# Score rows and centre norms from one product of the pooled sums, and a new order of every engine's list

## The chip, the cores and the metric

The kernel runs on one core of one Trainium2 chip. The metric is the device time of one execution in microseconds (us). The engines are TensorE (PE, with its weight loads shown apart as PEld), VectorE (DVE), ScalarE (ACT), GpSimd (POOL) and SyncE (SP, which issues the DMAs). They run their own instruction streams in order and meet at semaphores.

## The reference, cut to what matters

The input x has 32 images of 96 channels and 56 by 56 pixels. One layer is a clustering "convolution" and a quantised feed-forward part, each with a residual:

```
xn = x normalised over channels
f, v = Wf xn + bf, Wv xn + bv            # 8 heads of 48 channels
per quarter image (28x28 pixels) and head:
    centers = mean of f over 4x4 blocks of 7x7 pixels        # 16 centers
    cos(m, n) = f(n).centers(m) / (|f(n)| |centers(m)|)
    sim = sigmoid(beta + alpha * cos), kept for the best center of a pixel only
    agg(m) = (sum_n sim(m,n) v(n) + mean v) / (sum_n sim(m,n) + 1)
    out(n) = sum_m sim(m,n) agg(m)
x = x + Wp out + bp
t = x + FFN(normalised x)                # weights by sign, activations scaled by the
                                         # largest magnitude of a group of images
```

Pooling is linear, so the sums of xn over a block (with a constant row for the bias), call them s, give centers = Wf s. A score row is q = Wf^T (Wf s) = G s with G = Wf^T Wf for each head, and the squared length of a center is s^T G s = q.s. The groups of the feed-forward part are five groups of six images; the last two images have no feed-forward part.

## The kernel before, in words

A quarter image (784 pixels, 7 tiles of 112) is the unit of work. A group has 24 quarters. A first pass over them does the clustering part and the first half of the feed-forward part (normalise, transpose, the hidden product and its largest magnitude). When the largest magnitude of the whole group is known, a second pass over 48 half quarters recomputes the hidden product, applies GELU and the second weight, and leaves y on the chip. The final step of a group (clip y, scale it, add it to the image and store it) is done during the first pass of the next group. So the program is: setup, then five times a first and a second pass, then a last part with the eight quarters of the last two images and the final step of the fifth group. The final step is therefore in the first pass of groups 1 to 4 (counted from 0), and not in that of group 0.

The first pass is a software pipeline written by hand. `attention` of each engine is a list of steps, and `pipeline` runs the list once for each slot j. An entry is (phase, lag, step) and works on quarter j - lag + phase, with the phases X = 4 (normalise x, pool it, make score rows), M = 3 (features and their norms, scores), A = 2 (sigmoid, masking, aggregate, project, spread, residual) and R = 0 (feed-forward and final step). The order of the list is the order in which an engine issues. The entries marked FFN, FINAL and FILL are left out where a part has no such work.

For the score rows the kernel before goes this way: `pooled` (DVE) sums xn over blocks into cenx; `centers` (PE, L915) multiplies by wfT into 96 rows for each of four pairs of heads; `centers` (DVE, L656) copies that with a mask for the two heads into cbd; `center_squares` (POOL, L391) squares it into csq; `center_products` (PE, L923) sums the squares over rows by a product with ones and multiplies cbd by wf to get the 128 score rows; `center_floor` (DVE, L666), `center_norms` (POOL, L398), `q_scaled` (ACT, L491), `q_back` (PE, L950) and `q_placed` (ACT, L496) scale the rows by one over the length and turn them into Q; `scores` (PE, L967) uses Q one slot later. The four products of L930 each write 32 of the 128 output rows of a bank; `project` (L1007) does the same with eight products.

Other steps that the prediction speaks of: `features` (L954, seven tiles of 384 columns), `find_first` (L983), `sim_back` (L990), `aggregate` (L1000), `t_back` (L1027), `spread` (L1017), `x_back` (L904), `hidden_tiles` (L1045, six tiles, each emptied by `h_largest` on DVE), `to_tokens` (L883). `to_tokens("t")` of an even quarter waits for the `residual` of the next quarter, because a tile of tokens runs across two quarters of an image half: 

```
done(pe, "t_done", q + 1 - k % 2)
```

`moments` (POOL, L366) makes scale and shift from the statistics, `normalise` (ACT, L444) applies them to seven tiles. `marks` (POOL, L404) subtracts the maximum.

Of the kernel before, what the change touches and what calls it, by code (L numbers as in the profile page):

```python
# [14 lines left out]
T = QS // ROWS_T  # L15
# [21 lines left out]
POOL_SETS = 7  # L37
DVE_SUMS, DVE_SIGNS, DVE_ALL = 4, 20, 24
# [23 lines left out]
def build(nc, x, Wf, bf, Wv, bv, Wp, bp, alpha, beta, W1, b1, W2, b2, consts, out):  # L62
# [3 lines left out]
    with ctx:  # L66
# [53 lines left out]
        wf = sb("wf", [C, 4, C + 1])  # L120
# [34 lines left out]
        def early(rows, *shape):  # L155
# [12 lines left out]
        NAMES = """x_side x_T x_stats x_sum x_dif x_half x_d2 x_v x_var x_rstd x_shift x_norm0 x_norm xn_ps0 xn_ps xn_copied0 xn_copied cen_x cen_f cen_bd  # L168
            cen_sq q_ps cen_n2 cen_inv q_scaled q_T q_done s_ps n2_done n2_floor n_guess n_square n_part n_first n_second n_scaled n_factor
            n_inverse cos_done sig_done top_done eq_done  # L170
            eqT_ps eqT_copied first_ps sim_done simT_ps0 simT_ps simT_copied0 simT_copied u_ps u_done a_ps a_rden a_done o_ps0 o_ps t_done
            t_T t_stats t_sum t_dif t_half t_d2 t_v t_var t_rstd t_shift t_norm0 t_norm n_ps0 n_ps n_hi0 n_hi n_lo0 n_lo y_clip final""".split()
# [88 lines left out]
        def _(sp):  # L261
            per_row = [(cst[:, :], consts), (w1[:, :, :], W1[0:G1 * GROUPS, :].rearrange("(g r) c -> r g c", g=GROUPS)),
                       (w2[:, :, :], W2[0:G2 * GROUPS, :].rearrange("(g r) f -> r g f", g=GROUPS)),
                       (wf[:, :, 0:C], Wf.rearrange("(k r) c -> r k c", k=4)),
                       (wv[:, :, 0:C], Wv.rearrange("(k r) c -> r k c", k=4)),
                       (wf[:, :, C:C + 1], bf.rearrange("(k r a) -> r k a", k=4, a=1)),
# [85 lines left out]
        def _(pool):  # L352
# [6 lines left out]
            nc.gpsimd.memset(uT[:, :, :, :], 0.0).then_inc(pool_set, 1)  # L359
            pool.wait_ge(pool_set, POOL_SETS)  # L360

# [4 lines left out]
            def moments(s, eps):  # L366

                def step(k, q, place, use):
                    b = k % 2
                    a, w = st[s][:, b, :, :], mo[s][:, b, :, :]  # L370
                    done(pool, s + "_stats", q)
                    done(pool, s + "_norm", q - 2)
                    nc.gpsimd.tensor_tensor(w[:, 0:4:2, :], means(a, 1), means(a, 4), ALU.add).then_inc(S[s + "_sum"], 1)
                    nc.gpsimd.tensor_tensor(w[:, 1, :], a[:, :, 1], a[:, :, 4], ALU.subtract).then_inc(S[s + "_dif"], 1)
                    done(pool, s + "_sum", q)
                    nc.gpsimd.tensor_scalar(w[:, 6, :], w[:, 2, :], 1.0 / C, eps, ALU.mult, ALU.add).then_inc(S[s + "_v"], 1)
                    done(pool, s + "_dif", q)
                    nc.gpsimd.tensor_scalar(w[:, 3:5, :], w[:, 0:2, :], -0.5, 0.0, ALU.mult, ALU.add)\
                        .then_inc(S[s + "_half"], 1)
                    done(pool, s + "_half", q)  # L380
                    nc.gpsimd.tensor_tensor(w[:, 5, :], w[:, 4, :], w[:, 4, :], ALU.mult).then_inc(S[s + "_d2"], 1)
                    done(pool, s + "_v", q)
                    done(pool, s + "_d2", q)
                    nc.gpsimd.tensor_tensor(w[:, 7, :], w[:, 5, :], w[:, 6, :], ALU.add).then_inc(S[s + "_var"], 1)
                    done(pool, s + "_var", q)
                    nc.gpsimd.tensor_tensor(w[:, 8, :], w[:, 7, :], halfpow[0:TN, 0:T], ALU.pow).then_inc(S[s + "_rstd"], 1)
                    done(pool, s + "_rstd", q)
# [34 lines left out]
            def attention(g, part):  # L422
                return [(A, 0, marks), (X, 1, center_norms), (R, 0, clipped(g, part), FINAL),
                        (R, 0, moments("t", EPS_T), FFN), (X, 0, moments("x", EPS_C)), (X, 0, center_squares)]
# [18 lines left out]
        def _(act):  # L443
# [46 lines left out]

            def q_scaled(k, q, place, use):  # L491
# [4 lines left out]
            def q_placed(k, q, place, use):  # L496
                done(act, "q_T", q)
                done(act, "s_ps", q - 2)
                nc.scalar.copy(Q[:, k % 2, :], bank(0, C + 1, HM, 256)).then_inc(S["q_done"], 1)
# [39 lines left out]
            def attention(part):  # L539
                return [(X, 1, copy_x(1)), (A, 0, sigmoid), (M, 0, squares(0, 2)), (X, 0, gather),  # L540
                        (M, 0, squares(2, 4)), (X, 1, q_scaled), (A, 0, copy_eq), (M, 0, squares(4, 5)),
                        (X, 1, q_placed), (M, 0, squares(5, 7)), (A, 0, copy_sim(0)),
                        (R, 0, normalise("t", 6, 0), FFN), (R, 0, normalise("t", 6, 1), FFN),
                        (R, 0, n_high(0, part), FFN), (R, 0, n_high(1, part), FFN), (A, 0, copy_sim(1)),
                        (X, 0, normalise("x", 0, 0)), (X, 0, normalise("x", 0, 1)), (X, 0, copy_x(0)), (A, 0, shares)]
# [38 lines left out]
        def _(dve):  # L584
# [38 lines left out]
            for i in range(2):  # L623
                step(v.tensor_copy(V[:, 2 * i:2 * i + 2, :, 0:C],
# [11 lines left out]
            def stats(s, b0, g=0):  # L636
                def step(k, q, place, use):
# [3 lines left out]
                    done(dve, s + "_rstd", q - 2)  # L641
# [6 lines left out]
            def pooled(k, q, place, use):  # L648
# [4 lines left out]
                v.tensor_reduce(cenx[:, k % 4, :].rearrange("c (a b) -> c a b", a=4), blocks, AX.XY, ALU.add)\  # L653
# [12 lines left out]
            def center_floor(k, q, place, use):  # L666
                done(dve, "q_ps", q)
                done(dve, "cen_inv", q - 2)
                v.tensor_scalar(cn2[:, k % 2:k % 2 + 1], bank(0, HM, 1, 64), NORM_FLOOR * AREA * AREA, None, ALU.max)\
# [61 lines left out]
            def summed(k, q, place, use):  # L731
                done(dve, "u_ps", q)
                done(dve, "a_ps", q - 1)
                sums = cenx[:, k % 4, :].unsqueeze(1).broadcast_to([C + 1, HEADS, CENTERS])
# [79 lines left out]
            def attention(g, part):  # L814
                return [(M, 1, cosine), (R, 1, h_largest(2, 3), FFN), (X, 1, pooled), (R, 1, h_largest(3, 4), FFN),
                        (A, 0, maxima), (X, 1, centers), (R, 1, h_largest(4, 6), FFN), (A, 1, residual(0)),
                        (A, 1, residual(1)), (X, 1, center_floor), (R, 0, stats("t", 6, g), FFN), (M, 0, norms(0, TA)),
# [3 lines left out]
                        (R, 0, h_largest(0, 2), FFN), (A, 0, denominators)]  # L821
# [35 lines left out]
        def _(pe):  # L857
# [5 lines left out]
            mm(bank(1, G2, GROUPS), ones[0:G2, 0:G2], wsum2[:, :], start=True, stop=True)  # L863
            for k in range(4):
                tr(bank(2, C + 1, C, k * C), wf[:, k, :], ident[0:C, 0:C])
# [3 lines left out]
            for k in range(4):  # L869
                mm(bank(4 + k // 2, C + 1, 2 * C, k % 2 * 2 * C), wv[:, k, :],  # L870
                   wph[:, k, :, :].rearrange("r h o -> r (h o)"), start=True, stop=True)
            for g in range(GROUPS):
# [77 lines left out]
            def q_back(k, q, place, use):  # L950
                done(pe, "q_scaled", q)
                tr(bank(0, C + 1, HM, 256), qT[:, :], ident).then_inc(S["q_T"], 1)
# [102 lines left out]
            def attention(g):  # L1055
                return [(A, 1, project), (X, 1, x_back(0)), (R, 1, hidden_tiles(2, 3), FFN), (X, 1, x_back(1)),
                        (R, 1, hidden_tiles(3, 4), FFN), (A, 1, spread(0)), (R, 1, hidden_tiles(4, 5), FFN),
                        (A, 1, spread(1)), (X, 1, centers), (R, 1, hidden_tiles(5, 6), FFN), (M, 0, features(0, 2)),
# [73 lines left out]
```

## Time and profile before

| | us |
|---|---|
| runs | 3008.85, 3002.17, 3002.28; median 3002.28 |
| profiled execution, its own time | 3013.11 |
| its span, first to last instruction | 3011.3 |
| mean granted TensorE clock, share of full | 0.988 |
| busy: PE / DVE / ACT / POOL | 2836.4 / 2695.2 / 2246.1 / 1561.1 |

The page gives busy times over the whole span. The chain of waits is the sequence of instructions that ended last, followed back from the end: a piece of it is work that had nothing to hide behind. A window table gives busy times in a stretch. In a timeline row the first number is the start in us from the start of the span, the second the time taken, and brackets hold the idle time before it with what ended it.

### The profile page before, as it was taken

How to read it: one execution, taken by the hardware profiler on the slowest of the kernel's cores; microseconds unless marked ns; L12 is line 12 of the kernel's file. 1: busy time of each engine (PE TensorE's matmuls, PEld its weight loads, DVE VectorE, ACT ScalarE, POOL GpSimd, SP SyncE). 2: the span in 40 equal slices, each digit the busy share in tenths (PEclk: the TensorE clock that was granted, in tenths of full speed). 3: DMA queues.
4: the chain of work that ended last, by engine and by line, in shares of the span. 5: the costliest groups of instructions: out<-in, count | busy, mean ns of one | idle time of the engine just before them, and what ended most of it. 6: DMA issues, size and time to landing. Idle time of an engine off the chain costs nothing.

```text
span 3011.3 us, 62497 instructions
## 1 busy us (share of the span) xinstructions
PE 2836.4 (94%) x20998; PEld 1931.7 (64%) x20998; DVE 2695.2 (90%) x6308; ACT 2246.1 (75%) x4894; POOL 1561.1 (52%) x2739
## 2 busy tenths in 40 slices
PE   3999999999999999999999999999999999999987
PEld 2666666656666666666666556666665666666555
DVE  3689989899999989999999999999989999998976
ACT  2577777897777779777777987777779777777963
POOL 1344444575555543455555665555543555554854
PEclk9899999999999999999999999999999999999989
DMA  1011111002222210122222002222210222221025
GB/s 45 17 34 34 33 41 34 9 17 66 66 65 66 65 49 1 49 65 66 66 65 58 25 17 65 65 71 73 69 33 3 72 72 66 66 65 50 1 73 153
DMA packets 30930, 154.27 MB, mean 51 GB/s; under 512 B 6483, under 2 KB 6804, under 8 KB 30612
## 3 DMA queue, kind: packets, MB, share of 16 engines
q1 hardware_dynamic: 30612, 150.28, 18.0%
q8 instruction: 169, 2.77, 0.4%
q14 instruction: 149, 1.22, 0.1%
HBM read 75.60 MB, written 74.66 MB: 50 GB/s over the span
## 4 chain that ended last, share of the span: by engine, by line
PE 68%; ACT 15%; POOL 6%; issue 6%; DVE 5%; SPq 0%; DMA 0%; POOLq 0%; DVEq 0%; ACTq 0%
PE ps L963 20%; PE ps L1040 10%; ACT nT L457 9%; PE ps L1023 6%; PE ps L971 6%; PE ps L900 5%; PE ps L911 4%; ACT turns L560 4%; POOL turns L433 4%; PE ps L1096 3%; PE ps L919 3%; PE ps L1033 2%; DVE turns L838 2%; PE ps L1013 2%; PE ps L987 2%
## 5 line engine op out<-in xcount | busy, mean ns | idle before, releaser
L488 ACT ACTIVATE sq<-ps 112x384 f32<-112x384 f32 x896 | 444.8, 497 | 562.5 <-PE ps L963 547.6
L963 PE MATMUL ps<-wfT,xn 97*112 97x384 f32 x1792 | 736.4, 509 | 3.1 <-ACT sq L488 3.1
L1040 PE MATMUL ps<-tok,w1T 98*128 98x392 f16 x2880 | 617.9, 330 | 8.9 <-ACT turns L563 8.7
L396 POOL TENSOR_TENSOR csq<-cbd 96x128 f32<-96x128 f32 x128 | 50.6, 396 | 803.9 <-DVE cbd L662 803.9
L433 POOL CAST turns<-turns 128x392 f16<-128x392 f32 x240 | 319.8, 1346 | 205.1 <-ACT turns L560 201.1
L678 DVE TENSOR_REDUCE n<-sq 112x32 f32<-112x1536 f32 (+1 forms) x256 | 395.2, 1544 | 22.5 <-ACT sq L488 22.3
L1040 PEld LDWEIGHTS ps<-tok,w1T 98*128 98x128 f16 x2880 | 277.2, 100 | 182.9 <-issue 52.9
L769 DVE TENSOR_REDUCE hmax<-ps 128x1 f32<-128x392 f32 x720 | 380.8, 556 | 3.4
L457 ACT ACTIVATE xnT<-ps,mo_x 112x96 f32<-112x96 f32 x896 | 302.8, 442 | 98.1 <-POOL mo_x L388 98.1
L838 DVE SCALAR_TENSOR_TENSOR turns<-turns 128x1176 f16<-128x1176 f32 x240 | 331.0, 1379 | 0.0
L560 ACT ACTIVATE turns<-ps,scale 128x1176 f32<-128x1176 f32 x240 | 323.2, 1346 | 2.2 <-DVE scale L792 1.1
L963 PEld LDWEIGHTS ps<-wfT,xn 97*112 97x112 f32 x1792 | 272.5, 181 | 79.9 <-ACT sq L488 8.4
L1096 PE MATMUL ps<-turns,w2T 128*96 128x392 f16 x1440 | 288.4, 337 | 23.0 <-DVE turns L838 22.3
L457 ACT ACTIVATE nT<-ps,mo_t 112x96 f32<-112x96 f32 x840 | 284.3, 448 | 0.0
L1003 PE MATMUL ps<-sim,xnT 112*97 112x128 f32 x1792 | 228.1, 280 | 42.5 <-ACT turns L525 42.4
L644 DVE BATCH_NORM_STATS2 st_t<-ps 112x6 f32<-112x96 f32 x840 | 150.3, 251 | 111.1 <-PE ps L900 111.1
L1096 PEld LDWEIGHTS ps<-turns,w2T 128*96 128x96 f16 x1440 | 160.2, 123 | 135.1 <-DVE turns L838 91.7
L1003 PEld LDWEIGHTS ps<-sim,xnT 112*97 112x97 f32 x1792 | 200.6, 165 | 69.4 <-ACT turns L525 69.4
L408 POOL TENSOR_TENSOR eq<-sig,top 112x896 bf16<-112x896 f32 x128 | 219.1, 1712 | 48.4 <-DVE top L722 48.4
L1023 PE MATMUL ps<-turns,aggp 128*96 128x448 f32 (+1 forms) x512 | 219.3, 513 | 2.4 <-ACT aggp L504 1.7
L971 PE MATMUL ps<-Q,xn 97*112 97x128 f32 x1792 | 217.0, 273 | 0.6 <-ACT sq L488 0.6
L971 PEld LDWEIGHTS ps<-Q,xn 97*112 97x112 f32 x1792 | 203.3, 177 | 1.5 <-ACT sq L488 1.2
(140 smaller groups left out, 5859.9 us busy)
## 6 DMA issues: line engine op xcount, KB each, us to landing
xbuf<-in_x SPq DMA_DIRECT2D x64, 588.0 KB, 4.8
out<-xbuf SPq DMA_DIRECT2D x64, 588.0 KB, 6.0
turns<-out SPq DMA_DIRECT2D x60, 588.0 KB, 6.4
out<-turns SPq DMA_DIRECT2D x60, 588.0 KB, 4.4
tok<-in_L_ffn_W SPq DMA_DIRECT2D x2, 142.5 KB
cst<-in_constants SPq DMA_DIRECT2D x1, 195.0 KB
wf<-in_L_conv_Wf SPq DMA_DIRECT2D x1, 144.0 KB
tok<-in_L_conv_Wv SPq DMA_DIRECT2D x1, 144.0 KB
```

Source lines behind the costliest of these rows:

```text
L433: nc.gpsimd.tensor_copy(ghi[:, k % 3, HT:2 * HT], gel[:, k % 3, HT:2 * HT]).then_inc(b_mid, 1)
L457: ins = nc.scalar.activation(dst, bank(b0 + part, TN, C, (t - t0) * C), ACT.Identity, bias=m[:, 9, t:t + 1], scale=m[:, 8, t:t + 1])
L488: nc.scalar.activation(sq[:, t, :], bank(2 + t % 2, TN, D), ACT.Square).then_inc(f_sq, 1)
L560: nc.scalar.activation(gel[:, k % 3, :].rearrange("p (c n) -> p c n", c=FC), ps[:, h:h + 3, 0:HT], ACT.Gelu, scale=scale[:, 0:1]).then_inc ...
L678: ins = v.reduce_sum(n2[:, t0 * HEADS:t1 * HEADS], sq[:, t0:t1, :].rearrange("p t (h d) -> p (t h) d", d=HD), AX.X)
L838: v.scalar_tensor_tensor(glo[:, k % 2, :], gel[:, k % 3, :], QCLIP, ghi[:, k % 3, :], ALU.min, ALU.subtract).then_inc(b_lo, 1)
L963: mm(bank(2 + t % 2, TN, D), xn[:, k % 2, t * TN:(t + 1) * TN], wfT[:, :], start=True, stop=True)\
L971: ins = mm(tile_bank(2, TN, HM, t), xn[:, k % 2, t * TN:(t + 1) * TN], Q[:, k % 2, :], start=True, stop=True)
L1003: ins = mm(bank(4, C + 1, HM), xnT[:, k % 4, t, :], sim[:, k % 2, t * HM:(t + 1) * HM], start=t == 0, stop=t == T - 1)
L1023: mm(bank(4 + part, C, hi - lo), aggp[:, :], simT[:, lo:hi], start=True, stop=True)\
L1040: ins = mm(dst, w1T[:, c * 128:(c + 1) * 128], tok[:, bass.ds(place, 1), part, s * HT:(s + 1) * HT].rearrange("p a n -> p (a n)"), start=p ...
L1096: ins = mm(bank(6 + k % 2, C, HT), w2T[:, c, :], part[:, s, c * HT:(c + 1) * HT], start=n == 0, stop=n == 2 * FC - 1)
```

## The change: what it does

Setup: wf is loaded with one head in 48 rows. PE makes eight products of a head's wf with itself (48 rows, 97 by 97 outputs), and DVE copies them into G, beside a unit matrix of 97 by 97 for each head.

In the first pass the products of wfT with cenx, the masked copy, the squares and the product with ones are gone. `center_products` takes the pooled sums themselves, padded by 16 zeros on either side, as stationary operand of 32 columns, and [G | unit] of a head as 194 moving columns: eight products, two for each block of 32 output rows, one for each head of the pair. The result has 97 columns of score rows (G s) and 97 columns of the sums s turned into rows. A new ACT step `copy_products` copies the first half to qU, and a new DVE step `center_dots` multiplies it by the second half and adds along the row; `center_floor` then reads that sum.

The lists: `attention` of PE, ACT, DVE and POOL begin at another point of the cycle (with lag 1 where it was lag 0) and have some entries exchanged. Read as cycles, PE has `hidden_tiles` 0, project, 1 to 2, `x_back(0)`, `spread(0)`, `x_back(1)`, 3, `spread(1)`, `features(0,1)`, 4 to 5, `features(1,2)`, `center_products`; before it was 0 to 1, project, `x_back(0)`, 2, `x_back(1)`, 3, `spread(0)`, 4, `spread(1)`, `centers`, 5, `features(0,2)`, `center_products`. DVE takes h_largest 1 and 2, `residual(0)` and h_largest 3 ahead of `pooled`. ACT takes `shares` between the two halves of `normalise("x")`, and `squares(4,5)` behind `q_placed`. The small steps of `moments` count on one semaphore where each had its own; their instructions are the same. Eight transposes of 48 rows replace four of 96 in setup.

```diff
+            def copy_products(k, q, place, use):
+                done(act, "q_ps", q)
+                done(act, "cen_dot", q - 1)
+                nc.scalar.copy(qU[:, :], bank(0, HM, C + 1, 128)).then_inc(S["q_side"], 1)
...
-            def centers(k, q, place, use):
-
-                done(dve, "cen_f", q)
-                done(dve, "q_ps", q - 2)
-                f = bank(0, C, 4 * CENTERS).rearrange("r (k m) -> r k m", k=4)
-                mask = const("head_of_row", C)
-                v.tensor_tensor(cbd[:, k % 2, :, :, :], f.unsqueeze(2).broadcast_to([C, 4, 2, CENTERS]),
-                                mask.unsqueeze(1).unsqueeze(3).broadcast_to([C, 4, 2, CENTERS]), ALU.mult)\
-                    .then_inc(S["cen_bd"], 1)
+            def center_dots(k, q, place, use):
+                b = k % 2
+                done(dve, "q_side", q)
+                done(dve, "cen_n2", q - 2)
+                v.tensor_tensor_reduce(cprod[:, :], bank(0, HM, C + 1, 128 + C + 1), qU[:, :], 1.0, 0.0, ALU.mult, ALU.add,
+                                       accum_out=cdot[:, b:b + 1]).then_inc(S["cen_dot"], 1)
...
-            def center_squares(k, q, place, use):
-                b = k % 2
-                done(pool, "cen_bd", q)
-                done(pool, "q_ps", q - 2)
-                v = cbd[:, b, :, :, :].rearrange("c k h m -> c (k h m)")
-                nc.gpsimd.tensor_tensor(csq[:, b, :], v, v, ALU.mult).then_inc(S["cen_sq"], 1)
...
-            def centers(k, q, place, use):
+            def center_products(k, q, place, use):
                 done(pe, "cen_x", q)
                 done(pe, "xn_copied", q)
-                for c in range(4):
-                    ins = mm(bank(0, C, CENTERS, c * CENTERS), wfT[:, c * C:(c + 1) * C], cenx[:, k % 4, :],
-                             start=True, stop=True)
-                ins.then_inc(S["cen_f"], 1)
-
-            def center_products(k, q, place, use):
-
-                done(pe, "cen_bd", q)
-                done(pe, "cen_sq", q)
-                mm(bank(0, HM, 1, 64), csq[:, k % 2, :], ones[0:C, 0:1], start=True, stop=True)
-                n = 2 * CENTERS
-                for c in range(4):
-                    ins = mm(ps[c * n:(c + 1) * n, 0, 128:128 + C + 1],
-                             cbd[:, k % 2, c, :, :].rearrange("r h m -> r (h m)"), wf[:, c, :], start=True, stop=True)
+                n, turned = 2 * CENTERS, cenx[:, k % 4, :, :].rearrange("c s m -> c (s m)")
+                for h in range(2):
+                    for c in range(4):
+                        ins = mm(ps[c * n:(c + 1) * n, 0, 128:128 + 2 * (C + 1)], turned[:, (1 - h) * CENTERS:(1 - h) * CENTERS + n],
+                                 G[:, 2 * c + h, :, :].rearrange("c s o -> c (s o)"), start=h == 0, stop=h == 1)
                 ins.then_inc(S["q_ps"], 1)
...
+            step(v.tensor_copy(G[:, :, 1, :], ident[0:C + 1, 0:C + 1].unsqueeze(1).broadcast_to([C + 1, HEADS, C + 1])))
...
+            for h in range(HEADS):
+                mm(bank(h // 4, C + 1, C + 1, h % 4 * (C + 1)), wf[:, h, :], wf[:, h, :], start=True, stop=True)
```

## Rows read from the trace of the kernel before

**Rows 1.** The page, chain that ended last, shares by engine.

```profile
PE 68%; ACT 15%; POOL 6%; issue 6%; DVE 5%; SPq 0%; DMA 0%; POOLq 0%; DVEq 0%; ACTq 0%
```

**Rows 2.** Windows, one slot of group 1: length, then busy of each engine.

```profile
799.08:817.46 18.38, 17.88 (x143) 12.54 (x142) 17.06 (x45) 13.57 (x33) 10.04 (x20) 1.00 0.22 67
```

**Rows 3.** Chain of waits, the same slot: start, time, what.

```profile
799.25 0.61 PE ps L919 x8
...
801.49 0.12 PE ps L927 x2
801.61 0.30 PE ps L930 x8
801.91 0.83 PE ps L963 x2
...
808.50 2.38 ACT nT L457 x7
...
811.41 1.53 PE ps L971 x14
...
813.61 0.47 PE ps L1013 x16
...
814.10 0.63 PE ps L911 x4
...
815.07 0.53 PE ps L911 x3
...
817.62 0.61 PE ps L919 x8
```

**Rows 4.** Chain of waits, one slot of group 0.

```profile
300.70 0.61 PE ps L919 x8
...
315.54 0.56 PE ps L911 x4
316.09 0.33 PE ps L1040 x2
316.42 0.29 PE ps L911 x3
...
318.85 0.61 PE ps L919 x8
```

**Rows 5.** Timeline, VectorE in the slot of group 1.

```profile
801.22 1.15 DVE L750 SCALAR_TENSOR_TENSOR xbuf<-ps,bpc,xbuf 96x448 f32<-96x448 f32 x2
...
803.36 1.25 DVE L644 BATCH_NORM_STATS2 st_t<-ps 112x6 f32<-112x96 f32 x7 [0.93 <-PE ps L900]
...
813.31 1.04 DVE L769 TENSOR_REDUCE hmax<-ps 128x1 f32<-128x392 f32 x2
```

**Rows 6.** Groups by line: count, busy us, mean ns of one, idle before.

```profile
L1013 PE MATMUL ps<-V,uT 97*32 97x97 f32 x2048 | 69.6, 253 | 3.8 <-DVE uT L735 3.8
L493 ACT ACTIVATE qT<-ps,cinv 128x97 f32<-128x97 f32 x128 | 43.2, 337 | 27.9 <-POOL cinv L402 27.9
L662 DVE TENSOR_TENSOR cbd<-ps,cst 96x128 f32<-96x128 f32 x128 | 35.5, 277 | 9.5 <-PE ps L919 9.5
```

**Rows 7.** Timeline, setup.

```profile
33.43 2.88 PE L870 MATMUL ps<-tok 96*97 96x192 f32 x8 [13.30 <-DVE w1T L620]
...
39.88 1.15 DVE L624 COPY V<-ps 97x384 f32<-97x384 f32 x2 [6.50 <-PE ps L875]
```

**Rows 8.** Windows over the second passes of groups 0 and 1.

```profile
543.61:677.60 133.99, 123.42 (x736) 74.57 (x737) 124.62 (x200) 121.41 (x182) 93.44 (x69) 1.00 0.04 11
1100.27:1230.24 129.97, 123.17 (x736) 75.36 (x737) 120.19 (x202) 117.11 (x182) 43.95 (x69) 0.99 0.09 24
```

**Rows 9.** Timeline, one slot of the last part.

```profile
2953.34 1.09 DVE L722 TENSOR_REDUCE top<-sig 112x56 f32<-112x896 f32 x1
...
2956.18 0.40 POOL L396 TENSOR_TENSOR csq<-cbd 96x128 f32<-96x128 f32 x1 [7.36 <-DVE cbd L662]
2956.53 1.71 POOL L408 TENSOR_TENSOR eq<-sig,top 112x896 bf16<-112x896 f32 x1
```

More of the change, by code:

```diff
@@ L422, in attention @@
             def attention(g, part):
-                return [(A, 0, marks), (X, 1, center_norms), (R, 0, clipped(g, part), FINAL),
-                        (R, 0, moments("t", EPS_T), FFN), (X, 0, moments("x", EPS_C)), (X, 0, center_squares)]
+                return [(X, 1, moments("x", EPS_C)), (A, 0, marks), (X, 1, center_norms),
+                        (R, 0, clipped(g, part), FINAL), (R, 0, moments("t", EPS_T), FFN)]
             def group(g, part):
@@ L498, in q_placed @@
                 done(act, "s_ps", q - 2)
-                nc.scalar.copy(Q[:, k % 2, :], bank(0, C + 1, HM, 256)).then_inc(S["q_done"], 1)
+                nc.scalar.copy(Q[:, k % 2, :], bank(0, C + 1, HM, 352)).then_inc(S["q_done"], 1)
             def shares(k, q, place, use):
@@ L539, in attention @@
             def attention(part):
[L540 to L545, printed above, removed]
+                return [(M, 1, squares(4, 7)), (A, 1, copy_sim(0)), (R, 1, normalise("t", 6, 0), FFN),
+                        (R, 1, normalise("t", 6, 1), FFN), (R, 1, n_high(0, part), FFN), (R, 1, n_high(1, part), FFN),
+                        (A, 1, copy_sim(1)), (X, 1, normalise("x", 0, 0)), (A, 1, shares),
+                        (X, 1, normalise("x", 0, 1)), (X, 1, copy_x(0)), (X, 1, copy_x(1)), (A, 0, sigmoid),
+                        (M, 0, squares(0, 2)), (X, 0, gather), (X, 1, copy_products), (M, 0, squares(2, 4)),
+                        (X, 1, q_scaled), (A, 0, copy_eq), (X, 1, q_placed)]
             act.wait_ge(w_loaded, 16 * LOADS)
@@ L623, in _ @@
             for i in range(2):
+                step(v.tensor_copy(G[:, 4 * i:4 * i + 4, 0, :],
+                                   bank(i, C + 1, 4 * (C + 1)).rearrange("c (h o) -> c h o", h=4)))
+            step(v.tensor_copy(G[:, :, 1, :], ident[0:C + 1, 0:C + 1].unsqueeze(1).broadcast_to([C + 1, HEADS, C + 1])))
+            for i in range(2):
                 step(v.tensor_copy(V[:, 2 * i:2 * i + 2, :, 0:C],
@@ L871, in _ @@
                    wph[:, k, :, :].rearrange("r h o -> r (h o)"), start=True, stop=True)
+            for h in range(HEADS):
+                mm(bank(h // 4, C + 1, C + 1, h % 4 * (C + 1)), wf[:, h, :], wf[:, h, :], start=True, stop=True)
             for g in range(GROUPS):
@@ L1055, in attention @@
             def attention(g):
-                return [(A, 1, project), (X, 1, x_back(0)), (R, 1, hidden_tiles(2, 3), FFN), (X, 1, x_back(1)),
-                        (R, 1, hidden_tiles(3, 4), FFN), (A, 1, spread(0)), (R, 1, hidden_tiles(4, 5), FFN),
-                        (A, 1, spread(1)), (X, 1, centers), (R, 1, hidden_tiles(5, 6), FFN), (M, 0, features(0, 2)),
-                        (X, 1, center_products), (M, 0, features(2, 3)), (R, 0, to_tokens("t", 6, g), FFN),
-                        (M, 0, features(3, 4)), (A, 0, marks_back), (X, 1, end_of_group(g), FFN),
-                        (M, 0, features(4, 5)), (X, 1, q_back), (M, 0, features(5, 6)), (A, 0, find_first),
-                        (X, 0, to_tokens("x", 0)), (M, 0, features(6, 7)), (A, 0, sim_back(0)), (A, 0, sim_back(1)),
-                        (A, 0, aggregate), (R, 0, t_back(0), FFN), (A, 1, fill(2), FILL), (X, 1, fill(2), FILL),
-                        (R, 0, t_back(1), FFN), (M, 0, scores), (R, 0, hidden_tiles(0, 2), FFN)]
+                return [(M, 1, features(5, 6)), (A, 1, find_first), (X, 1, to_tokens("x", 0)), (M, 1, features(6, 7)),
+                        (A, 1, sim_back(0)), (A, 1, fill(2), FILL), (A, 1, sim_back(1)), (A, 1, aggregate),
+                        (R, 1, t_back(0), FFN), (R, 1, t_back(1), FFN), (X, 1, fill(2), FILL), (M, 1, scores),
+                        (R, 1, hidden_tiles(0, 1), FFN), (A, 1, project), (R, 1, hidden_tiles(1, 3), FFN),
+                        (X, 1, x_back(0)), (A, 1, spread(0)), (X, 1, x_back(1)), (R, 1, hidden_tiles(3, 4), FFN),
+                        (A, 1, spread(1)), (M, 0, features(0, 1)), (R, 1, hidden_tiles(4, 6), FFN),
+                        (M, 0, features(1, 2)), (X, 1, center_products), (M, 0, features(2, 3)),
+                        (R, 0, to_tokens("t", 6, g), FFN), (M, 0, features(3, 4)), (A, 0, marks_back),
+                        (X, 1, end_of_group(g), FFN), (M, 0, features(4, 5)), (X, 1, q_back)]
             def column_to_row(n, i):
```

74 lines of the change are left out of this document (38 added, 36 removed).

## The prediction

> **What bounds the kernel now.** I read the page's chain first [rows 1]: PE carries 68% of it and no other engine comes near, so PE's issue order sets the end. The windows of one slot of the first pass say by how much [rows 2]: in 18.38 us PE is busy 17.88 and DVE 17.06, ACT 13.57, POOL 10.04. The reader is to see that DVE has little more room than PE: an order that frees PE helps only until DVE is full.
>
> Then the chain through one slot, in order of time. It comes round at the first L919 after 18.37 us in a group with the final step [rows 3] and after 18.15 us in group 0 without it [rows 4]. There are 24 slots in each of five groups; one of each group is broken by the second pass, so I count 23 intervals per group: 92 of 18.37 and 23 of 18.15. The second passes take the rest and the change doesn't touch their steps. From one masked step to the next across it they take 134.0 or 130.0 us [rows 8]; POOL is busy 93 us in one and 44 in the other with the same 69 instructions, so the same code runs there in two ways. The profiled execution (3013.1) is 10.8 us above the median of the runs (3002.3), about what a few groups in the longer way would cost; I carry savings over to the median as they are and put such a swing into the range.
>
> **The change part by part.**
>
> *PE, removed.* In the chain the step `centers` costs 0.61, the sum of squares 0.12 and the four products 0.30 [rows 3]: 1.03 us of each slot.
>
> *PE, added.* Eight products of 194 columns run as 16 passes. What a column costs I take from the scores: 14 passes of 128 columns in 1.53 us (L971, [rows 3]), 0.109 a pass or 0.85 ns a column, so 0.082 us for 97 columns and 0.165 for 194. One after the other 16 passes would be 2.64 us. But `project` has the same shape with 97 columns: its 16 passes last 253 ns each on average [rows 6], 4.0 us in sum, and stand in the chain with 0.47 [rows 3]. So passes that write different 32 output rows run at the same time. Four side by side, 16 passes are 4 x 0.082 = 0.33, which leaves 0.14 for starting. For the new step: 4 x 0.165 + 0.14 = 0.80. Bounds: 0.65 (starting hidden) and 2.78 (no overlap). I take 0.80, since the nearest row has the same count, the same 32 columns and the same order of blocks. PE net: 0.80 - 1.03 = -0.23.
>
> One rule speaks against it. In the trace the 16 weight loads and 16 passes of `project` fit into 0.47 us [rows 3]. The Trainium skill, "TensorE: Matmul & The Clock Gate", Part 3 (packing small matmuls), says that a weight load overlaps running matmuls only if it goes to other row groups; here all blocks use the same rows. By that rule each of the four rounds would also pay a load of about 0.11 us, for the new step 1.24 instead of 0.80. The same sum for `project` gives 0.91, and the trace has 0.47: it doesn't agree. I keep 0.80 and give the rule a small chance below.
>
> *PE, order.* In group 1 the seven tiles of `x_back` take 0.63 + 0.53 = 1.16 in the chain [rows 3], in group 0 0.56 + 0.29 = 0.85 [rows 4]. The difference, 0.31, is a wait for the normalised x. In the new order hidden tiles 1 and 2 (0.33 each, L1040 [rows 4]) stand before `x_back(0)`, so it starts about 0.33 later, at 811.41 + 1.53 + 0.47 + 3 x 0.33 = 814.4 against 814.10, and `spread(0)` instead of one hidden tile stands before `x_back(1)`. I expect the 0.31 to vanish: 18.37 - 0.23 - 0.31 = 17.83. Against that `shares` goes between the halves of `normalise("x")`, which makes the second half later by about 0.34 (a row of that kind, L493 [rows 6]); `x_back(1)` comes about 0.4 later, so it fits narrowly. The long wait before `scores` (the 2.38 of ACT's normalise [rows 3], behind which most of `aggregate` hides) stays.
>
> *DVE.* The masked copy, 0.277 [rows 6], goes; `center_dots` comes. No row shows a multiply with a sum along the row. Lower bound 0.277, the same size from the same bank without the sum; upper 0.55, as if the sum were a second pass. I take 0.30. So DVE's work stays at 17.1. What can be late is the residual: today it starts in the chain's clock at 801.22 and ends at 802.37 [rows 5], just before PE wants it for `to_tokens("t")`. DVE runs from its hidden tile at 813.31 to that end one slot on, 820.74, in 7.43. The new list does the same work there without the masked copy (0.28), with a few waits less, so the residual ends some 0.3 to 0.4 earlier; PE gets there 0.5 earlier. For even quarters that is a wait of 0.1 to 0.2; odd quarters don't wait. I add 0.1 on average: **17.93**. `center_dots` itself sits where DVE waits 0.93 for tokens today [rows 5], so its cost and the wait for `copy_products` are hidden there; without that cover each slot pays 0.3. Behind it on DVE stand the statistics, the norms and the masking: that chain ends at `masked`, which `sim_back` on PE waits for.
>
> *ACT and POOL.* `copy_products` is one copy of 128 x 97, 0.34 by the scaling of the same rows [rows 6]; ACT has 18.38 - 13.57 = 4.8 us of room a slot. POOL loses the 0.40 of squares [rows 9]. The merged semaphores remove no instruction.
>
> *The turn of the lists.* Moving the start of a list while changing lags leaves the same sequence, also at the edges: before a second pass the same steps have run as before. I cost it at nothing. At an edge the score-row chain is bare: before 0.61 + 0.28 + 0.40 + 0.42 = 1.71, now 0.80 + 0.34 + 0.30 = 1.44, so 0.3 at each of five edges: 1.5.
>
> *Group 0.* No wait at `x_back` there, so 18.15 - 0.23 = 17.92.
>
> *Last part.* POOL's `marks` stands behind the squares: the maximum is there at 2953.34 + 1.09 = 2954.43, marks start at 2956.53 [rows 9]. Without the squares they can start 2.1 earlier; PE's own queue will eat part. Some five slots, 1 us each: 5 (bounds 0 and 10).
>
> *Setup.* Sixteen more passes of 97 columns: L870 has 2.88 / 8 = 0.36 for 192 columns there [rows 7], so 16 x 0.18 = 2.9. Three more copies in a row on DVE: two as L624, 1.15 [rows 7], and one of twice the columns, at most as long as both; I take 1.0. Four more transposes, at most 0.18 each: 0.7. Nothing covers this: +5.7 (bounds 3.5 and 7).
>
> **The sum.** 92 x (18.37 - 17.93) = 40.5; 23 x 0.23 = 5.3; edges 1.5; last part 5; setup -5.7: 46.6 us saved. Against the profiled execution's own time: 3013.1 - 46.6 = 2966.5. Against the median: 3002.3 - 46.6 = **2955.7**, 2956.
>
> **The rivals.**
>
> *Deeper gain* (0.15). The even-quarter wait doesn't occur and the loosened order removes part of the waits before `scores` too; PE falls to 17.65 in both kinds of slot. 92 x 0.72 + 23 x 0.5 + 1 = 79: 2924. For it: PE's wait for the 2.38 of ACT's normalise is still there to be filled [rows 3]. Against: DVE, at 17.1, would be 97% busy.
>
> *DVE takes over* (0.20). `center_dots` costs 0.55 and DVE keeps its waits of about 0.9 [rows 5] at other places: 17.06 - 0.28 + 0.55 + 0.9 = 18.2. Saved: 92 x 0.17 + 1 = 17: 2986. For it: DVE is 93% busy now. Against: its one long wait is exactly where the new step goes.
>
> *The wait only moves* (0.07). `x_back(1)` waits behind `shares`, `q_back` behind the longer row chain; the slot stays at about 18.3. 6 saved, setup already paid: 2996 to 3002, no change.
>
> *The loads don't overlap* (0.03). The new step costs 1.24, slot 18.37, group 0 18.36: 23 x 0.21 = 5 lost, 1 gained elsewhere: 3006. That is the rule of the Trainium skill above.
>
> *The passes don't overlap at all* (0.05), the other side. Then the product costs 2.78, net +1.75 a slot, less the 0.31: 92 x 1.44 + 23 x 1.75 = 173: 3175. It turns from gain to loss once the product costs more than 1.03 + 0.31 = 1.34 us. For it: the moving operand is twice as wide as any that the trace shows in this form, and all four blocks use one stationary operand. Against: `project`.
>
> My forecast has 0.50.
>
> **How the numbers follow.** A measurement here tells about 0.3%, 9 us, from no change: faster means under 2993, slower over 3011. Faster: 0.50 + 0.15 + most of the DVE case (0.17) = 0.82. Same: 0.03 + 0.06 + 0.02 = 0.11. Slower: 0.07. The range takes in the deeper gain and the DVE case with a few us for the two ways of the second pass: 2922 to 2992. The likeliest case alone: 2943 to 2968 (slot 17.85 to 18.05, last part 0 to 10).
>
> **What would show it.** The chain of a slot should come round after 17.9 us, with one piece of about 0.80 for the 16 passes of the new product where 1.03 stood, and `x_back` near 0.85. DVE's idle before the statistics of t should fall from 0.93 to a few tenths, and `center_dots` stand at about 0.3. A product of 1.2 or more, a DVE step of more than 0.5, or a chain that goes through DVE between the hidden tiles and the residual would make the forecast wrong. A total off by steps of about 4 us with the slots as forecast is the second pass.

## The result, and the profile after

The changed kernel takes 2925.86 us (median of 4 runs, 2924.38 to 2933.98) against 3002.23 (4 runs, 3001.98 to 3008.85) beside it: a ratio of 0.9746, interval 0.9724 to 0.9768, or 76 us. The forecast was 47, its range held the time. The profiled execution took 2924.38, its span 2922.6, at a mean granted clock of 0.992.

The page's chain by engine, after; it answers to [rows 1].

```profile
PE 71%; ACT 12%; issue 6%; POOL 6%; DVE 5%; SPq 0%; DMA 0%; DVEq 0%; POOLq 0%; ACTq 0%
```

Windows of two slots of group 1, an odd and an even quarter (length, then busy of PE, PEld, DVE, ACT, POOL, then clock), after; they answer to [rows 2].

```profile
779.51:797.15 17.64, 17.19 (x141) 11.43 (x140) 17.07 (x47) 13.88 (x34) 9.74 (x20) 1.00 0.36 104
797.15:814.93 17.78, 17.34 (x142) 11.80 (x143) 17.07 (x47) 13.88 (x34) 9.74 (x20) 1.00 0.13 35
```

DVE's 17.07 is what it was. PE's busy time fell by 0.6 and its idle time stayed near 0.45: almost nothing was gained as idle time, so the pieces themselves must be shorter. The chain of waits through these slots, after, against [rows 3]:

```profile
779.51 0.58 PE ps L904 x7
...
782.96 0.58 PE ps L904 x7
...
784.20 0.56 PE ps L991 x4
...
785.21 2.38 ACT nT L451 x7
...
789.99 0.47 PE ps L1008 x16
790.47 0.77 PE ps L1035 x4
791.24 0.39 PE ps L915 x4
791.62 0.75 PE ps L1018 x2
792.38 0.29 PE ps L915 x3
...
795.52 0.80 PE ps L925 x16
...
797.15 0.72 PE ps L904 x7
```

Three pieces of the chain before that stand beside them: the transposes of x's tokens, `sim_back`, and two hidden tiles.

```profile
806.22 0.76 PE ps L900 x7
...
807.65 0.40 PE ps L996 x4
...
812.94 0.66 PE ps L1040 x4
```

The new product (L925) is 0.80 where 0.61, 0.12 and 0.30 stood. `x_back` (L915) is 0.39 + 0.29 = 0.68 where 0.63 + 0.53 stood. Tokens of x (L904, second row) are 0.58 for 0.76, and `sim_back` (L991) is 0.56 for 0.40. Tokens of t (L904, first and last row) are 0.58 in one slot and 0.72 in the next. ACT's normalise, 2.38, stays. Sum: -0.23 - 0.48 - 0.18 + 0.16 + 0.07 (half of 0.14) = -0.66, which is 18.37 less the mean of 17.64 and 17.79. The pieces left out of this sum cancel: the six hidden tiles take 2.10 for 2.00, since the two that now stand behind `project` (L1008, L1035) take 0.77, where two take 0.66 or 0.67 elsewhere; both `spread` take 1.32 for 1.36, and "issue" 0.47 for 0.53.

DVE's timeline at the even quarter, after (start, time; idle before it in brackets), answers to [rows 5]; behind it stand the groups of the new steps (busy, mean ns), which answer to L662 in [rows 6].

```profile
796.48 0.55 DVE L751 SCALAR_TENSOR_TENSOR xbuf<-ps,bpc,xbuf 96x336 f32<-96x336 f32 x1
796.95 0.26 DVE L663 CUSTOM_DVE_ANT_0 cprod<-ps,qU 128x97 f32<-128x97 f32 x1
797.13 0.08 DVE L663 DVE_READ_ACCUMULATOR2_ANT cdot<- 128x1 f32 x1
...
797.91 1.25 DVE L647 BATCH_NORM_STATS2 st_t<-ps 112x6 f32<-112x96 f32 x7 [0.50 <-PE ps L904]
```

```profile
L663 DVE CUSTOM_DVE_ANT_0 cprod<-ps,qU 128x97 f32<-128x97 f32 x128 | 33.2, 259 | 5.8 <-ACT qU L488 5.8
L488 ACT COPY qU<-ps 128x97 f32<-128x97 f32 x128 | 30.3, 237 | 12.9 <-PE ps L925 12.9
```

`center_dots` is two records, 0.26 and 0.08, about 0.30 from start to start of what follows; the wait before the statistics of t fell from 0.93 to 0.50 (even) and 0.36 (odd).

The spans differ by 3011.3 - 2922.6 = 88.7. I split that at the masked step, once per quarter:

| part | forecast | measured |
|---|---|---|
| setup | -5.7 | -6.2 |
| fill, to the third masked step | 0 | +14.5 |
| 23 slots of group 0 | 5.3 | 10.0 |
| 92 slots of groups 1 to 4 | 40.5 | 60.7 |
| second passes and edges | 1.5 | 3.4 |
| last part | 5 | 6.3 |

The medians differ by 76.4 only, since the profiled execution before was 10.9 above its median and that after 1.5 below. The masked steps don't say where in the program that excess lay, so a part in the table may hold some of it; the slots of groups 1 to 4 before, alike within 0.09 us, hold little.

Two parts hold a surprise. Windows over the fill, before and after:

```profile
80.00:100.00 20.00, 18.04 (x105) 12.16 (x104) 11.76 (x27) 9.01 (x21) 4.31 (x11) 0.76 0.00 1
100.00:126.20 26.20, 24.22 (x158) 15.65 (x157) 14.84 (x37) 15.12 (x34) 8.13 (x19) 0.83 0.08 24
```

```profile
80.00:100.00 20.00, 18.25 (x134) 11.56 (x127) 12.96 (x34) 12.58 (x30) 7.37 (x12) 0.89 0.00 1
100.00:117.80 17.80, 16.39 (x137) 11.03 (x136) 14.53 (x37) 12.33 (x30) 6.35 (x16) 1.00 0.12 35
```

And over the first slot of the last part, before and after:

```profile
2899.34:2923.16 23.82, 20.77 (x119) 13.80 (x118) 15.50 (x33) 10.77 (x25) 11.08 (x15) 0.71 0.44 127
```

```profile
2816.90:2835.10 18.20, 16.05 (x125) 10.85 (x124) 15.55 (x34) 10.79 (x26) 8.69 (x12) 1.00 0.45 122
```

In both, the granted clock (third number from the end) is part of the gain. Before, it was 0.76 and 0.83 on average in the fill and 0.71 in that slot, mixtures of its lower level (0.5, 1.2 GHz) and 1.00 (2.4 GHz). Before, it fell to 0.50 at 95.0 us, behind 10.2 us in which PE was busy 8.24, and was back at 108.7. After, no such fall comes in the fill: it is at 1.00 from 84.2 us on, and at 1.00 in the slot. About the same number of matmuls then takes less: 119 took 20.77 us at 0.71, 125 take 16.05 at 1.00. This isn't a trait of the profiled execution before alone: its mean granted clock was 0.988, and the 27 executions of the kernel before in the sets of runs below had 0.985 to 0.990, those of the changed kernel 0.992 or 0.993.

### The profile page after: what moved, and what is told of

The parts are those of the page before. It is cut to its first block, busy times and chain, and to the rows that moved or that the text cites. A ratio compares the mean times of both kernels' runs of the same rounds, so it can differ in the third digit from the quotient of the medians.

```text
span 2922.6 us, 61782 instructions
## 1 busy us (share of the span) xinstructions
PE 2755.8 (94%) x20762; PEld 1809.3 (62%) x20762; DVE 2701.7 (92%) x6439; ACT 2286.0 (78%) x5022; POOL 1525.9 (52%) x2612
## 4 chain that ended last, share of the span: by engine, by line
PE 71%; ACT 12%; issue 6%; POOL 6%; DVE 5%; SPq 0%; DMA 0%; DVEq 0%; POOLq 0%; ACTq 0%
PE ps L958 20%; PE ps L1035 13%; ACT nT L451 9%; PE ps L966 6%; PE ps L1018 5%; PE ps L1091 5%; PE ps L904 5%; POOL turns L427 4%; PE ps L925 3%; PE ps L915 3%; PE ps L991 2%; ACT turns L559 2%; PE ps L1028 2%; PE ps L1008 2%; DVE turns L839 2%
## 5 line engine op out<-in xcount | busy, mean ns | idle before, releaser
L958 PE MATMUL ps<-wfT,xn 97*112 97x384 f32 x1792 | 747.5, 504 | 3.1 <-ACT sq L482 3.1
L482 ACT ACTIVATE sq<-ps 112x384 f32<-112x384 f32 x896 | 428.9, 498 | 380.7 <-PE ps L958 364.7
L1035 PE MATMUL ps<-tok,w1T 98*128 98x392 f16 x2880 | 599.7, 330 | 8.7 <-ACT turns L562 8.6
L451 ACT ACTIVATE xnT<-ps,mo_x 112x96 f32<-112x96 f32 x896 | 315.9, 433 | 105.9 <-POOL mo_x L389 105.9
L1035 PEld LDWEIGHTS ps<-tok,w1T 98*128 98x128 f16 x2880 | 268.3, 97 | 203.2 <-issue 28.1
L770 DVE TENSOR_REDUCE hmax<-ps 128x1 f32<-128x392 f32 x720 | 380.4, 555 | 3.4
L451 ACT ACTIVATE nT<-ps,mo_t 112x96 f32<-112x96 f32 x840 | 284.3, 448 | 0.0
L1018 PE MATMUL ps<-turns,aggp 128*96 128x448 f32 (+1 forms) x512 | 212.3, 496 | 3.3 <-ACT aggp L503 3.3
L387 POOL TENSOR_TENSOR mo_x<-mo_x,halfpow 112x7 f32<-112x7 f32 x128 | 192.8, 1506 | 10.0
```

The costliest lines, as they stand in the source:

```text
L451: ins = nc.scalar.activation(dst, bank(b0 + part, TN, C, (t - t0) * C), ACT.Identity, bias=m[:, 9, t:t + 1], scale=m[:, 8, t:t + 1])
L482: nc.scalar.activation(sq[:, t, :], bank(2 + t % 2, TN, D), ACT.Square).then_inc(f_sq, 1)
L770: v.tensor_reduce(o, bank(6 + u % 2, 128, HT), AX.X, ALU.max, apply_absolute_value=True)\
L958: mm(bank(2 + t % 2, TN, D), xn[:, k % 2, t * TN:(t + 1) * TN], wfT[:, :], start=True, stop=True)\
L1035: ins = mm(dst, w1T[:, c * 128:(c + 1) * 128], tok[:, bass.ds(place, 1), part, s * HT:(s + 1) * HT].rearrange("p a n -> p (a n)"), start=p ...
```

## The experiments

The kernel before had medians of 3002 to 3010 in the four sets of runs, while the changed kernel and two variants with nearly its slots lie between 2919.55 and 2925.86; so all are compared by their slot lengths (mean over 92 slots of groups 1 to 4) and own medians beside the ratios.

### Which half of the change gave it

Old rows in the new lists, and new rows in the old lists. The steps that the other half lacks are put in: `centers` before features 1 and 2 in the new lists; `copy_products` behind `gather` and `center_dots` before `center_floor` in the old ones. PE's entries, the first against the changed kernel, the second against the kernel before:

```diff
-   (M, 0, features(1, 2)), (X, 1, center_products), (M, 0, features(2, 3)),
+   (X, 1, centers), (M, 0, features(1, 3)), (X, 1, center_products),
```

```diff
-   (X, 1, centers), (R, 1, hidden_tiles(5, 6), FFN), (M, 0, features(0, 2)), (X, 1, center_products),
+   (R, 1, hidden_tiles(5, 6), FFN), (M, 0, features(0, 2)), (X, 1, center_products),
```

> The new lists with the score rows and norms made as before (centers, masked copy, squares, product of ones). The steps of the old way stand where the new product stood: centers before features 1 and 2, center_products after them. Theory, the gain is two separate parts: the order alone gives about 0.43 us a slot and the product about 0.23, so the slot of groups 1 to 4 comes round in 17.95 us, group 0 in about 17.9, and the whole is 2955 to 2965 us. Rival, the order pays only with the new product, because the masked copy and the squares stand between: slot 18.2 or longer, whole 2985 or more.

Measured: 2974.42 us, ratio 0.9892 (0.9877 to 0.9907); slots of 17.95 and 18.03. The slots are near those that the theory gave (17.95), the whole is 9 us above its range; in the profiled execution the five second passes sum to 677.1, against 665.1 before.

> The new product, copy and dot with the lists of before (copy_products behind gather, center_dots before center_floor). Theory of two parts: slot of groups 1 to 4 18.14 us, group 0 17.92, the fill of the pipeline before the third masked step shorter by some 10 us because features no longer stand behind centers and so behind pooled; whole 2960 to 2970. Rival, the time the product gives back is lost again at the next wait (x_back for the normalised x): slot 18.3 or more, whole 2980 to 2990.

Measured: 2990.81 us, ratio 0.9946 (0.9931 to 0.9961); slots of 18.29, 17.99 in group 0. In groups 1 to 4 the rival came out.

| slot, groups 1 to 4 (group 0) | old lists | new lists |
|---|---|---|
| old rows | 18.38 (18.15) | 18.00 (17.99) |
| new rows | 18.29 (17.99) | 17.72 (17.71) |

Alone the rows give 0.09 and the lists 0.38; together 0.66. In the old lists PE does get the 0.23 of the product, but meets a new wait. The chain with new rows in old lists:

```profile
835.75 0.62 PE ps L915 x4
...
836.72 0.53 PE ps L915 x3
...
839.27 0.49 PE ps L1035 x2
...
841.05 0.80 PE ps L925 x16
```

The last hidden tile (L1035) takes 0.49, every other one 0.33. It follows `spread(1)` directly now that the 0.61 of `centers` is gone from between, and waits for the maximum that empties its bank (DVE's ends at 839.2); that gives back 0.16 of 0.23. In the new lists DVE takes its maxima earlier and no hidden tile takes 0.49 there. The old rows cost 1.07 in these lists and the product 0.80; the slot falls by 0.28 (18.00 to 17.72), with the features 0.11 longer and the tokens of t 0.07 to 0.14 shorter. What was forecast as one kernel-wide sum was two edits that need each other.

### Do passes side by side depend on the order of blocks

```diff
-   for h in range(2):
-       for c in range(4):
+   for c in range(4):
+       for h in range(2):
```

> The changed kernel with the eight products in the other order: both heads of a block of 32 rows one behind the other, then the next block. Theory, passes run side by side only when they write different blocks of rows: the product's piece in the chain grows from 0.80 to about 1.4 us (eight turns of 0.165 and the start), the slot to 18.3, the whole by about 70 us to 2995. Rival, the side by side running does not depend on the order of the blocks: 0.80, and no change of the whole.

Measured: 2919.55 us, ratio 0.9708 (0.9692 to 0.9724), slots of 17.66 and 17.79; the piece in the chain:

```profile
809.32 0.82 PE ps L925 x16
```

My theory falls: the order in which blocks are issued doesn't matter. In the records, here too the 16 passes start in four rounds of four, at 809.25, 809.44, 809.60 and 809.77, as those of the changed kernel do at 795.45, 795.64, 795.81 and 795.97. The rounds are 0.16 to 0.19 apart, near the 0.165 that the prediction took for 194 columns. Which block a pass writes isn't in the records, so that the four of a round write four different blocks isn't contradicted, and not shown either. The 6 us between the medians of this and the changed kernel aren't in the slots (the spans of the profiled executions differ by 3.0); the five second passes sum to 657.7 here and to 661.7 there.

### Is the product's length still on the path

```diff
-   for h in range(2):
+   for h in (0, 1, 0, 1):
```

> The eight products of center_products are issued twice, the second time over the first, so that PE has four more rounds of four passes: 4 x 0.165 = 0.66 us more in each slot. Theory: in the new order PE sets the length and DVE follows (0.36 to 0.50 us of waits left before the statistics of t), so all of it lands on the slot: 18.3 to 18.45, some 125 slots x 0.66 = 80 us more, 2995 to 3010. Rival, other engines hold part of the slot and PE has room beside the chain: slots of 17.9 to 18.1, 2945 to 2975.

Measured: 2996.65 us, ratio 0.997 (0.9957 to 0.9984); slots of 18.31, the piece 1.46 for 32 passes. So 0.66 more of product is 0.67 more of slot in odd quarters and 0.52 in even ones, where the 0.14 of wait for the residual covers some. It also bounds the point where gain turns to loss: with 1.46 the kernel still stands 0.3% under the one before; the prediction had put the turn at 1.34.

### Is center_dots hidden

```diff
+   v.tensor_tensor_reduce(cprod2[:, :], bank(0, HM, C + 1, 128 + C + 1), qU[:, :], 1.0, 0.0, ALU.mult, ALU.add,
+                          accum_out=cdot2[:, :])
    v.tensor_tensor_reduce(cprod[:, :], ...
```

> The changed kernel with the product and sum of center_dots done twice on DVE, the first time into a place that nothing reads. It costs 0.34 us a slot on DVE (0.26 and 0.08 in the trace). Theory, as predicted: center_dots lies in DVE's wait for the tokens of t, of which 0.36 (odd quarters) to 0.50 us (even) is left; a second one just fits, slots stay within 0.05, 2924 to 2932. Rival, DVE has become the bound (92% busy): the whole 0.34 comes on top, slots of 18.05, 2960 to 2970.

Measured: 2922.47 us, ratio 0.9704 (0.9684 to 0.9725), slots of 17.64 and 17.79 as in the changed kernel. DVE's timeline at an odd quarter, a row of the changed kernel first, then rows of this one:

```profile
780.12 1.25 DVE L647 BATCH_NORM_STATS2 st_t<-ps 112x6 f32<-112x96 f32 x7 [0.36 <-PE ps L904]
```

```profile
814.96 0.26 DVE L664 CUSTOM_DVE_ANT_0 cprod<-ps,qU 128x97 f32<-128x97 f32 x1
...
815.15 0.25 DVE L666 CUSTOM_DVE_ANT_0 cprod<-ps,qU 128x97 f32<-128x97 f32 x1
...
815.78 1.25 DVE L648 BATCH_NORM_STATS2 st_t<-ps 112x6 f32<-112x96 f32 x7 [0.18 <-PE ps L907]
```

The wait before the statistics took it up: 0.36 to 0.18 in odd quarters, 0.50 to 0.33 in even ones. So the second product and sum cost 0.17 to 0.18 there, as their starts lie 0.19 apart, and not the 0.34 expected; no slot grew by it. DVE, busy 92% of the span, is still not the bound at this place.

### Which exchange in the lists mattered

First the old order of hidden tiles on PE with the old order of maxima, `pooled` and `residual` on DVE, all else new:

```diff
-   (R, 1, hidden_tiles(0, 1), FFN), (A, 1, project), (R, 1, hidden_tiles(1, 3), FFN), (X, 1, x_back(0)), (A, 1, spread(0)), (X, 1, x_back(1)),
+   (R, 1, hidden_tiles(0, 2), FFN), (A, 1, project), (X, 1, x_back(0)), (R, 1, hidden_tiles(2, 3), FFN), (X, 1, x_back(1)),
...
-   [(R, 1, h_largest(1, 3), FFN), (A, 1, residual(0)), (R, 1, h_largest(3, 4), FFN), (X, 1, pooled),
+   [(R, 1, h_largest(2, 3), FFN), (X, 1, pooled), (R, 1, h_largest(3, 4), FFN),
...
-   (R, 0, h_largest(0, 1), FFN), (A, 0, denominators), (M, 0, cosine)]
+   (R, 0, h_largest(0, 2), FFN), (A, 0, denominators), (M, 0, cosine)]
```

> The changed kernel with the order of before among hidden tiles, x_back and spread on PE and among hidden maxima, pooled and residual on DVE; ACT and POOL as changed. Theory, the wait of x_back for the normalised x (0.31 to 0.48 us a slot) comes back: slot 18.0 to 18.2, whole 2960 to 2980. Rival, the order on ACT made the gain (shares and q_placed earlier): slot below 17.85, whole under 2945.

Measured: 3081.13 us, ratio 1.0247 (1.0232 to 1.0262), slots of 19.00: slower than the kernel before, though PE's and DVE's orders here are its own. Both theory and rival missed. The chain of this kernel:

```profile
1285.74 0.29 DVE uT L736
...
1288.09 0.81 DVE hmax L770 x2
...
1288.96 0.17 DVE rden L742
1289.15 0.03 ACT aggp L503
1289.17 0.21 issue
1289.39 1.08 ACT xnT L451 x3
...
1290.51 0.53 PE ps L915 x3
```

The reader is to see a ring through three engines. DVE takes two maxima (L770) before the reciprocal (L742); ACT's `shares` (L503) waits for that; the second half of normalise x (L451) stands behind `shares`; `x_back(1)` (L915) waits for it, and so on to DVE's next slot. To test the ring, `shares` alone went back to its old place, in this kernel and in the changed one:

```diff
-   (X, 1, normalise("x", 0, 0)), (A, 1, shares), (X, 1, normalise("x", 0, 1)), (X, 1, copy_x(0)),
+   (X, 1, normalise("x", 0, 0)), (X, 1, normalise("x", 0, 1)), (X, 1, copy_x(0)), (A, 1, shares),
```

> The kernel with the earlier order of hidden tiles on PE and of maxima, pooled and residual on DVE, in which a slot lasted 19.0 us, and in it shares back behind copy_x(0) on ACT. Theory: the 19.0 came from a ring through three engines: shares waits for the reciprocal on DVE, which stands behind one more maximum there; the second half of normalise x waits behind shares, x_back(1) for it, and pooled on DVE for x_back(1). With shares out of the way the ring is open: slots of 18.0 to 18.3, 2960 to 2990. Rival, the order of DVE's list alone (both residuals behind the maxima) makes the 19.0: slots of 18.8 or more, 3055 or more.

Measured: 2981.15 us, ratio 0.9903 (0.9882 to 0.9924), slots of 18.29.

> One entry of ACT's list of the changed kernel goes back to where it was before: shares stands behind copy_x(0) and not between the halves of normalise x. Theory: spread(0) now stands ahead of x_back(1) on PE and needs shares, so this move is what the new order of PE lives on; with shares some 1.4 us later, spread(0) waits about 1 us, and x_back(1) and the pooled sums behind it: slots of 18.4 to 18.8, 3006 to 3045. Rival, by my prediction's reading (the move only costs the second half of normalise 0.34): slots of 17.6 to 17.8, 2915 to 2930.

Measured: 3056.45 us, ratio 1.016 (1.0122 to 1.0197), slots of 18.76. Its chain, with `spread(0)` (L1018) behind `shares` and `x_back(1)` behind that:

```profile
843.43 0.37 ACT aggp L503
843.80 0.04 issue
843.84 0.99 PE ps L1018 x2
844.84 0.29 PE ps L915 x3
```

| slot, groups 1 to 4 | old order of PE and DVE | new order |
|---|---|---|
| `shares` behind copy_x(0) | 18.29 | 18.76 |
| `shares` between the halves | 19.00 | 17.72 |

Either exchange alone costs 0.5 to 0.7 a slot, both together gain 0.57.

`q_placed` ahead of the squares of tile 4 is the exchange that shortened the tokens of x:

```diff
-   (M, 1, squares(4, 7)), ..., (A, 0, copy_eq), (X, 1, q_placed)]
+   (M, 1, squares(5, 7)), ..., (A, 0, copy_eq), (M, 0, squares(4, 5)), (X, 1, q_placed)]
```

> One entry of ACT's list of the changed kernel goes back: squares of tile 4 stand ahead of q_placed again. In the chain to_tokens of x fell from 0.76 to 0.58 with the change, and sim_back rose from 0.40 to 0.56. Theory: q_placed is late for to_tokens of x again (0.76), and sim_back, which waits for the masked step on DVE, gives it back (0.40): slots within 0.05 of the changed kernel's 17.64 and 17.79, 2918 to 2930. Rival, the two waits have nothing to do with each other: slots 0.18 longer, 2940 to 2950.

Measured: 2934.12 us, ratio 0.977 (0.9753 to 0.9787); slots of 17.70 and 17.85, 0.06 longer each (0.05 was allowed, and the time is 4 us above the range). In the chain the tokens of x are 0.76 again and `sim_back` is 0.40 again: the -0.18 and the +0.16 above are one wait in two places, worth 0.06 with 0.03 of issue time.

### An attempt to go further

```diff
-   (A, 0, maxima), (R, 1, h_largest(4, 6), FFN), (A, 1, residual(1)),
+   (A, 0, maxima), (A, 1, residual(1)), (R, 1, h_largest(4, 6), FFN),
```

> One entry of DVE's list of the changed kernel is moved: residual(1) stands ahead of h_largest(4, 6) and no longer behind it. Theory: slots of even quarters are 0.15 us longer (17.79 against 17.64) only because two maxima of about 0.5 us stand ahead of the residual that to_tokens of t waits for. The spread that residual(1) reads ends about 2 us before DVE comes to this point, so nothing new waits; all slots then last 17.64 to 17.66, some 60 x 0.15 = 9 us less, 2914 to 2920. Rival, DVE is full and only its order changes: the two maxima then push center_dots and the statistics back, the slots stay at 17.7 in the mean and the time at 2923 to 2929.

Measured: 2937.99 us, ratio 0.9756 (0.9737 to 0.9776); all slots 17.85. The even quarters no longer differ, but every slot is a little longer than the worse one (17.79). DVE's timeline and the chain of this kernel:

```profile
800.18 0.55 DVE L751 SCALAR_TENSOR_TENSOR xbuf<-ps,bpc,xbuf 96x336 f32<-96x336 f32 x1
800.65 1.02 DVE L770 TENSOR_REDUCE hmax<-ps 128x1 f32<-128x392 f32 x2
```

```profile
801.79 0.03 issue
801.82 0.76 PE ps L904 x7
```

Both my theory and its rival missed: `to_tokens("t")` writes the banks of the hidden tiles, so it waits for the last maximum too, in every quarter. It needs both of the exchanged steps, and only their common end counts. With 0.03 of waiting and 0.76 the tokens of t cost 0.79 in every slot, 0.72 or 0.58 in the changed kernel. None of the kernels run here is clearly faster than the changed one.

## Why the prediction came out as it did

*PE's product* was right: 0.80 forecast and measured, and the four rounds stand in the records. The rule of the Trainium skill, "TensorE: Matmul & The Clock Gate", Part 3, that would have made it 1.24 doesn't agree with this trace: weight loads of the second round start at 795.479 to 795.499, while passes on the same 97 rows run from 795.453 to 795.805.

*PE's order* is a term that was mis-sized: 0.31 was forecast, and about 0.40 came. "I expect the 0.31 to vanish" took group 0's 0.56 + 0.29 = 0.85 as `x_back` without a wait. It held none, but 0.85 isn't the length in the new order. The weight loads (PEld) of `x_back(0)` before, in group 0 and in group 1:

```profile
315.46 0.44 PEld L911 LDWEIGHTS ps<-cst,xnT 112*97 112x97 f32 x4
```

```profile
814.10 0.44 PEld L911 LDWEIGHTS ps<-cst,xnT 112*97 112x97 f32 x4 [0.23 <-ACT xnT L457]
```

In group 1 the first load waits for ACT's normalise. In group 0 it doesn't: the four tiles that it needs were done at 314.98, 0.48 earlier. Yet the piece is 0.56 there, directly behind `project`, and 0.39 in the new order, behind a hidden tile. What a step pays for standing behind `project` hasn't gone: the hidden tiles stand there now and take 0.11 more (0.77 for 0.66). This is read from the rows; no run moved that place alone. So `x_back` gave 0.48 and 0.03 of visible waits, less 0.11: 0.40, which is 0.09 of the 0.22 a slot by which groups 1 to 4 beat the forecast (17.72 against 17.93). The rest are small terms that the prediction hadn't: `q_placed` gave 0.02 by the pieces and 0.03 of issue time (0.06 when put back alone), `spread` 0.04, and the even-quarter wait was 0.07 on average where I had 0.1.

In group 0 the 0.21 beyond the forecast is mostly a wait that it didn't look for: `spread(0)` waited for `shares` (its first weight load for 0.30, which ACT ended). It took 0.90 before and takes 0.75 now.

```profile
317.05 0.90 PE ps L1023 x2
```

"`x_back(1)` fits narrowly" behind `shares` was right, but I priced `shares` as a cost of 0.34 to normalise; the 2 x 2 table shows that the new order of PE needs it.

*The fill* was costed at nothing and gave 14.5. The cause is bounded, not separated: with the lists alone the fill shortens by 9.4, with the rows alone by 12.2, and in both the granted clock is 1.00 from 100 us on. With the new rows features no longer stand behind `centers`, which waited for `pooled`, and PE's clock comes back to 1.00 sooner; which of the two leads wasn't tried. The clock alone can't be all of it: before, it was 0.50 in the windows 71.1 to 84.8 and 95.0 to 108.7, 27.4 us, and after only in that of 74.0 to 84.2, 10.2 us. The 17.2 us less at half the clock are worth at most 8.6 (an estimate, with PE as the bound all that time), so 5.9 or more came otherwise; some of it may be the excess of the profiled execution before.

*DVE* was right: `center_dots` at 0.30 lies in the wait for tokens, and its double does too; the wait of even quarters, forecast at 0.1 to 0.2, was 0.14. *ACT*: `copy_products` is 0.237 for 0.34. *Setup*: 6.2 for 5.7; the 16 passes took 2.93 for 2.9.

*Last part*: 6.3 for 5, for another reason. The sum came from its first slot, 23.82 to 18.19, where the clock had been 0.71; the other four slots together gave 0.7. There 13.7 us stood at 0.50 (2907.6 to 2921.3), worth at most 6.9 by the same estimate, so the clock can be the whole of it; no run shows it apart. In the other four the earlier start of `marks` is worth next to nothing.

The time is that of the rival "deeper gain" (2924), but not by its mechanism: the even-quarter wait did occur, and the wait of 2.38 before `scores` is untouched. By its mechanism the case I had for likeliest was the right one, but the time lies outside the 2943 to 2968 that I gave for it: the order was 0.09 a slot too small, the small terms and the wait in group 0 were missing, and the fill was left out. That the whole range held the time is luck in so far as its lower end came from the rival.

## What to carry to other kernels

A wait can cost without showing idle time: pieces of the same instructions with two lengths in the chain (0.58 and 0.76, 0.29 and 0.53) are the sign, and the shortest length is the one to forecast with. Ask first whether the difference is a wait at all: part of it can belong to the place, as the 0.11 behind `project` did, and then the step that takes the place pays it. Exchanges in the issue orders of several engines can be one edit: `shares` on ACT and the order of PE and DVE were each a loss when made singly, and a gain together. Before moving a step ahead of another, list every wait of the step that is to gain; two producers on one engine give their common end, whatever their order.

## What the runs showed of the hardware

A late semaphore costs PE about 0.2 us beyond the wait: 0.18 for the seven transposes below, 0.24 for the three of `x_back(1)` before (0.53 in group 1, 0.29 in group 0 without the wait, both behind a hidden tile). PEld's timeline for the tokens of t, first in the changed kernel at an odd quarter, then in the kernel with the residual first:

```profile
779.03 0.13 PEld L904 LDWEIGHTS ps<-cst,xbuf 96*112 96x112 f32 x1 [0.15 <-issue]
```

```profile
801.79 0.60 PEld L904 LDWEIGHTS ps<-cst,xbuf 96*112 96x112 f32 x7 [0.63 <-issue]
```

Where the semaphore is there in time, the first weight load starts at 779.03, 0.48 before the piece begins in the chain at 779.51, under the products ahead. Where it isn't, load and start come after them: the chain has 0.03 of waiting, and 0.76 for the seven transposes in place of 0.58. Sixteen passes into four blocks of 32 output rows ran in four rounds of four in either order of issue. A product with a sum along the row leaves two records on DVE, 259 and 83 ns; the Trainium skill, "VectorE: DVE Perf Modes", "Two Vector instructions with no wait between them", says that an operation with an accumulator output is two instructions, and the trace agrees.
